# Conditional residual block on one core: means of three norms from rounded halves of their input

## What is computed

```python
x = x + conv(x, cond)            # causal, 32 taps per channel, the taps are the condition vectors
ada = cond @ ada_w + ada_b       # six parts: shift1, scale1, gate1, shift2, scale2, gate2, per batch
x1 = ln(x) * (1 + scale1) + shift1
q, k, v = split(x1 @ qkv_w + qkv_b)          # 16 heads of 128
o = softmax(q @ k.T * 128 ** -0.5) @ v       # within each batch of 32 tokens
x = x + gate1 * (o @ out_w + out_b)
x2 = ln(x) * (1 + scale2) + shift2
x = x + gate2 * (gelu(x2 @ ffn_w1 + ffn_b1) @ ffn_w2 + ffn_b2)
# ln(x) = (x - mean(x)) * rsqrt(var(x) + 1e-6), over the 256 channels
```

## Time and profile before

| what | value |
|---|---|
| median of three runs | 316.98 us |
| the profiled execution, its own time | 316.77 us |
| span of that execution, first to last instruction | 315.0 us |
| TensorE busy | 305.2 us, 97% |
| VectorE, ScalarE, GpSimd busy | 55%, 54%, 38% |
| TensorE on the chain that ended last | 91% |
| mean granted clock of TensorE | 0.991 of full speed |

### The profile page before, as it was taken

One profiled execution on the slowest core, in us unless ns is written; L12 is line 12 of the kernel. 1 busy time (PEld: TensorE's weight loads), 2 busy tenths in 40 slices (PEclk: granted clock), 3 DMA queues, 4 the chain that ended last, 5 costly groups with the idle time before them and its releaser, 6 DMA issues.

```text
span 315.0 us, 6111 instructions
## 1 busy us (share of the span) xinstructions
PE 305.2 (97%) x2595; PEld 256.7 (82%) x2595; DVE 173.1 (55%) x298; ACT 170.1 (54%) x305; POOL 120.2 (38%) x103
## 2 busy tenths in 40 slices
PE   4999999999999999999999999999999999999994
PEld 3896997988888878888887888888898888688883
DVE  3995698877867445553435653450720556555232
ACT  5572567433762657376356636744762794714900
POOL 5006729330822454064327123630912571611400
PEclk9998999999999999999999999999999999999998
DMA  7902322400070052007003400430070020000022
GB/s 214 382 14 76 113 81 63 140 0 0 5 267 0 2 176 92 1 4 262 5 3 115 153 2 2 156 112 0 20 249 2 2 67 0 3 0 2 0 67 68
DMA packets 14987, 23.00 MB, mean 73 GB/s; under 512 B 776, under 2 KB 8048, under 8 KB 14960
## 3 DMA queue, kind: packets, MB, share of 16 engines
q1 hardware_dynamic: 14912, 22.58, 21.1%
q10 hardware_dynamic: 48, 0.03, 0.0%
HBM read 21.57 MB, written 1.05 MB: 72 GB/s over the span
## 4 chain that ended last, share of the span: by engine, by line
PE 91%; DVE 4%; POOL 1%; ACT 1%; DMA 1%; issue 0%; DVEq 0%
PE bank L875 18%; PE bank L877 18%; PE bank L876 18%; PE bank L949 9%; PE bank L883 5%; PE bank L827 5%; PE bank L884 4%; PE bank L885 4%; PE bank L933 3%; PE bank L836 2%; PE bank L868 2%; POOL wl L273 1%; PE bank L861 1%; DVE xc L503 1%; DMA crow<-in_cond_dram 1%; DVE yacc L634 1%
## 5 line engine op out<-in xcount | busy, mean ns | idle before, releaser
L273 POOL TENSOR_TENSOR wl<-raw,wh 128x512 fp32r<-128x512 f32 x72 | 98.5, 1394 | 135.4 <-ACT wh L336 118.7
L380 ACT ACTIVATE pool<-bank,bT 128x512 f32<-128x512 f32 x56 | 38.5, 688 | 57.6 <-PE bank L877 57.6
L875 PE MATMUL bank<-x1h,wl 128*128 128x512 f32 (+1 forms) x176 | 67.6, 384 | 0.8 <-DVE x1l L572 0.4
L877 PE MATMUL bank<-x1h,wh 128*128 128x512 f32 (+1 forms) x176 | 65.2, 370 | 0.0
L876 PE MATMUL bank<-x1l,wh 128*128 128x512 f32 (+1 forms) x176 | 65.1, 370 | 0.0
L620 DVE SCALAR_TENSOR_TENSOR ol<-bank,bT,oh 128x512 fp32r<-128x512 f32 x32 | 24.0, 749 | 38.8 <-ACT oh L405 37.8
L503 DVE SCALAR_TENSOR_TENSOR xc<-x,condT,xc 128x496 f32<-128x496 f32 (+27 forms) x82 | 42.8, 591 | 0.1
L336 ACT ACTIVATE wh<-raw 128x512 fp32r<-128x512 f32 x72 | 40.9, 622 | 3.5 <-PE bank L877 3.5
L875 PEld LDWEIGHTS bank<-x1h,wl 128*128 128x128 f32 x176 | 33.2, 189 | 7.6 <-DVE x1l L572 0.9
L876 PEld LDWEIGHTS bank<-x1l,wh 128*128 128x128 f32 x176 | 33.2, 189 | 6.0 <-issue 0.7
L877 PEld LDWEIGHTS bank<-x1h,wh 128*128 128x128 f32 x176 | 33.1, 188 | 5.8
(11 more groups left out here) (102 smaller groups left out, 420.0 us busy)
## 6 DMA issues: line engine op xcount, KB each, us to landing
raw<-in_L_cond_qkv_w_dram SPq DMA_DIRECT2D x24, 512.0 KB, 5.5
raw<-in_L_cond_out_w_dram SPq DMA_DIRECT2D x8, 512.0 KB, 3.6
raw<-in_L_cond_ffn_w_dram SPq DMA_DIRECT2D x4, 512.0 KB, 5.0
adaw<-in_L_cond_ada_w_dram SPq DMA_DIRECT2D x1, 1024.0 KB, 9.9
out_dram<-pool SPq DMA_DIRECT2D x4, 256.0 KB, 2.2
pool<-in_x_dram SPq DMA_DIRECT2D x2, 256.0 KB, 3.1
adaw<-in_L_cond_ada_w_dram SPq DMA_DIRECT2D x1, 512.0 KB, 5.7
pool<-in_x_dram SPq DMA_DIRECT2D x1, 512.0 KB, 6.6
```

Source lines behind the costliest of these rows:

```text
L273: g.tensor_tensor(wl[:, cols], raw[:, cols], wh[:, cols].bitcast(F32), ALU.subtract)\
L380: a.activation((q_sb if j < GH else k_sb)[:, j % GH, :], src, ACT.Identity, bias=bias(U, j // GH, j % GH)).then_inc(s_ev, 1)
L875: pe.matmul(dst, wl[:, w_cols], a_hi, start=start, stop=False)
L877: return pe.matmul(dst, wh[:, w_cols], a_hi, start=False, stop=stop)
```

## The change

The means of norms 2, 3 and 4 are no longer made from float32 operands. ScalarE copies the norm's input to `x1h` as float32r (`mean_high`), VectorE subtracts that from the input and writes `x1l` (`mean_low`), and TensorE multiplies both with a rounded matrix of 1/256 (`ones_r`), in four float32r matmuls. The buffers `x1h` and `x1l` are free at that time and are overwritten by the norm's own result later. In the streams, `mean_high(2)` and `mean_high(3)` stand between `high_parts(U + 1, 1)` and `exps(U)` of units 2 and 4, and `mean_low(2)` and `mean_low(3)` ahead of `softmax_front` of the same unit. In the tail `mean_high(4)` stands between `hidden(0, 4)` and `hidden(0, 5)`, `mean_low(4)` between `residual(1)` and `hidden_low(0, 5)`, `mean(4)` moves behind tiles 6 and 7 of `ffn1`, `squares(4)` behind `hidden(0, 6)`, and `var(4)` and `spread(4)` each one k later.

```diff
+        ones_r = sb("ones_r", [P, P], F32R)
...
             a.activation(rs[:, :], mhalf[:, :], ACT.Copy)
+            a.activation(ones_r[:, :], ones[:, :], ACT.Copy).then_inc(s_ones_r, 1)
...
+            def mean_high(n):
+
+                for ct in range(CT):
+                    a.wait_ge(s_in, CT * n + ct + 1)
+                    a.activation(part(x1h, ct, NORMS[n]), ln_in(n, ct), ACT.Copy).then_inc(s_mhi, 1)
...
                 high_parts(U + 1, 1)
+                if U == 2:
+                    mean_high(2)
+                if U == 4:
+                    mean_high(3)
                 exps(U)
                 evac(U, 9)
...
             hidden(0, 4)
+            mean_high(4)
             hidden(0, 5)
+            hidden(0, 6)
             squares(4)
-            hidden(0, 6)
             hidden(0, 7)
...
+            def mean_low(n):
+                for ct in range(CT):
+                    v.wait_ge(s_mhi, CT * (n - 2) + ct + 1)
+                    v.tensor_tensor(part(x1l, ct, NORMS[n]), ln_in(n, ct),
+                                    part(x1h, ct, NORMS[n]).bitcast(F32), ALU.subtract).then_inc(s_mlo, 1)
...
             conv(1, 22, len(DVE_LAGS[1]))
+            mean_low(2)
             softmax_front(2)
...
             residual(0)
+            mean_low(3)
             softmax_front(4)
...
             residual(1)
+            mean_low(4)
             hidden_low(0, 5)
...
             def mean(n):
                 pe.wait_ge(s_const, 2)
+                if n >= 2:
+
+                    pe.wait_ge(s_ones_r, 1)
+                    pe.wait_ge(s_mlo, CT * (n - 1))
+                    for t in (x1h, x1l):
+                        for ct in range(CT):
+                            m = pe.matmul(STAT_BANK[n][:, :], ones_r[:, :], part(t, ct, NORMS[n]),
+                                          start=(t is x1h and ct == 0), stop=(t is x1l and ct == CT - 1))
+                    m.then_inc(s_mean, 1)
+                    return
...
-            ffn1(0, (4, 5))
+            ffn1(0, (4, 5, 6, 7))
             mean(4)
-            ffn1(0, (6, 7))
...
-                if k == 0:
+                if k == 1:
                     var(4)
-                if k == 2:
+                if k == 3:
                     spread(4)
```

More of the change, by code:

```diff
@@ L135, in cond_resid_block_kernel @@
         s_adap, s_adat = sem("ada_product"), sem("ada_steps")
+        s_ones_r, s_mhi, s_mlo = sem("ones_rounded"), sem("mean_input_high"), sem("mean_input_low")
         s_in, s_mean, s_xm, s_sq = sem("ln_input"), sem("ln_mean"), sem("ln_centred"), sem("ln_squares")
```

## The result

The changed kernel takes 320.07 us (median of six runs), 1.0084 of the kernel before (95% interval 1.0048 to 1.0119), which had a median of 317.42 beside it. That is 2.65 us more, and the interval goes from 1.5 to 3.8. The sum on record was 2.66 and the time forecast 319.5. That the two differences meet within 0.01 is luck: the kernel before had medians from 316.73 to 317.42 in the comparisons of this record.

What follows compares the result with a forecast made beforehand. The prediction took TensorE, busy 97% of the span, as the bound. Terms 1.42 + 1.42 - 0.18 = +2.66 us on the profiled 316.77 gave 319.4, put at 319.5 to compare with medians; 8-in-10 range 315.4 to 320.9.

Steps and rivals of the forecast that it cites:

- Cost of a mean, 1.72 before and 0.91 after: Means 2 and 3 on TensorE: four float32r matmuls take 0.91 us instead of 1.72, a gain of 0.81 each.
- Slack of 1.36 behind the exponential: Ahead of unit 3's tile 0: the exponential's chain may slip 1.36 us free; beyond that TensorE stalls, 2.06 us.
- the addition for tile 1: Tile 1 of unit 3: evac(2, 10) comes too late for TensorE's second matmul, adding 0.17 us to the stall.
- The collision and its alternation: `mean_low` and GpSimd's low parts exclude each other and take turns; in unit 2 the maximum slips 3.42 us.
- The form between: Only the first subtraction waits for GpSimd: sum -0.7, 316.1 us; 25% together with the rival of order without collision.
- Net +1.42 each in units 2 and 4: Each of these units costs 2.23 us in stalls and gains 0.81 from the cheaper mean: +1.42 net.
- Tail -0.18: Region of `mean(4)`: product 0.91 plus a stall of 1.39 make 2.30 us against 2.48 before, so -0.18.
- nothing is held: Rival: the exponential slips under 1.36 us, so all gains (0.81, 0.81, up to 1.57) come, 3.19 less: 313.6 us; 5%.

Runs made afterwards that it cites:

- e5: Changed kernel with the product of means 2, 3 and 4 in float32 as before, copies and subtractions made but unused: 322.91 us, 1.0174 of the kernel before.
- e1: Changed kernel with GpSimd held in units 2 and 4 until both `mean_low` subtractions are done: 317.51 us, 1.001 of the kernel before.
- e3: Changed kernel with GpSimd held in the tail until `mean_low(4)` is done, before the last two weight low parts: 320.87 us, 1.0094 of the kernel before.
- e4: e3 plus the copies of means 2 and 3 moved up behind evac(U, 5) on ScalarE: 314.57 us, 0.9914 of the kernel before.
- e7: e4 with GpSimd's tail reordered, one low part before and one after a wait for `scale_up(4)`: 313.58 us, 0.9893 of the kernel before.

## Why the prediction was right

- **Cost of a mean, 1.72 before and 0.91 after.** Right. e5 sets the difference at 0.81 and 0.82, unit 4 and tail.
- **Slack of 1.36 behind the exponential, then us for us.** Right in kind, and two small terms in it were off and cancelled. The 0.38 from a release to TensorE's second matmul was read behind a wait of 0.18 us. Behind the long waits here (0.59 to 1.85 us, in the changed kernel and e1) it was 0.45. So the second matmul of tile 0 came 2.13 later behind the start of the scores than before, for 2.06 on record (2.10 by the gap alone), and the addition for tile 1 was 0.10 (114.53 to 115.99, less six steps) for 0.17 on record. Both sums are 2.23. With e1's smaller slip the gap was 0.83 (0.82).
- **The collision and its alternation.** Right, and e1 shows it as the cause: with GpSimd out of the way the pair falls from 2.55 to 1.29. The maximum slipped by 3.44, forecast 3.42. The form between, with only the first subtraction waiting, did not occur. Two readings of Rows 9 were off without effect: the convolution ended at 100.42, two short steps after 100.10, and the twelve steps behind the meeting go from 112 columns down to 32. The pair alone at 1.29 (e1) shows the collision without them. Here the rule of the Trainium skill, "SBUF — State Buffer", section "Who interferes with whom", agrees with the trace: the later instruction is shut out, and in e3 and e4 the same happens to `scale_up`.
- **Net +1.42 each in units 2 and 4.** Measured +1.45 and +1.46.
- **Tail -0.18.** Measured -0.18. The wait shown is 1.19, forecast about 1.2. One meeting was not in the sum: `hidden_low(0, 5)` took 1.77 us beside GpSimd's L313. It held `centre(4)` until 279.11, 0.31 after the end of the mean's last matmul (278.80), where 0.04 was the distance before the change. TensorE then went through the variance and the spread without a wait, so it cost nothing there.
- **The rival "nothing is held" (-3.19).** Wrong for this change, and nearly true once the order is another: e7 shows 0.82, 0.82 and 1.39 in place of 0.81, 0.81 and 1.57.
- **What I did not see**: the same collision behind the mean, once GpSimd's work is delayed (e3). In the changed kernel `scale_up` does not meet it. That cost a wrong forecast of an experiment, 1.4 us for a measured 0.45.

## What to carry to other kernels

Price an added instruction by the stream position it takes, not by its duration alone: two copies and two subtractions cost 2.1 us of the bound engine, since they stood ahead of the one chain with some 1.3 us of slack and met GpSimd there (1.27 of the 2.1), and five microseconds earlier in the same streams they were free. Before putting a VectorE operation with two inputs in SBUF anywhere, look at what GpSimd does in that very microsecond, and when GpSimd's work is moved out of one meeting, follow it to the next. A cheaper product is worth its preparation only where that is hidden; in the tail the reordering alone gave 0.80 us, reordering and rounding together 0.18, and both together 1.39 once GpSimd was out of the way (e7).

## What was not expected of the hardware

In the profiled execution of e5, TensorE's clock fell to its lower level (1.2 of 2.4 GHz) for a while right behind the stall ahead of unit 3. The granted clock is the third number from the right.

```profile
112.00:113.00 1.00, 0.61 (x3) 0.56 (x4) 0.93 (x3) 1.00 (x3) 0.16 (x1) 1.00 0.00 0
114.00:115.00 1.00, 1.00 (x3) 0.77 (x3) 0.94 (x3) 1.00 (x3) 1.00 (x2) 0.50 0.00 0
```

```profile
112.39 0.47 PE L907 MATMUL bank<-x1h,wl 128*128 128x512 f32 x1 [1.85 <-ACT pool L392]
...
114.16 0.63 PE L907 MATMUL bank<-x1h,wl 128*128 128x512 f32 x1
114.58 0.63 PE L908 MATMUL bank<-x1l,wh 128*128 128x512 f32 x1
```

Matmuls then started 0.43 us apart instead of 0.23, and the stretch of unit 2 took 15.44 us where 13.95 (as in unit 4, after a stall of the same length, at full clock) was due: 1.5 us. The profiled executions of the changed kernel, e3 and e5 hold six stalls of this length, two each, and only this one was followed by a drop. Whether the stall brought it on is not shown, and no experiment was made on it. If it did, a stall can cost more than its length, in some executions.
